# Order of the first loads, patch norms and splits in the prologue of a vision tower kernel

## The reference, cut to what matters

```python
pe = jax.lax.conv_general_dilated(pixel_values, conv_w, (PS, PS), 'VALID', ...)
red = grid.mean(axis=(3, 5)).reshape(b, C, hw).transpose(0, 2, 1)
win = grid.transpose(0, 2, 4, 3, 5, 1).reshape(b, hw, N, C)
q = _ln(red, la_ln_q_g, la_ln_q_b) @ la_wq
kv = _ln(win, la_ln_kv_g, la_ln_kv_b) @ la_wkv
...
local_out = red + agg @ la_proj_w + la_proj_b
```

## Time and profile before

| | us |
|---|---|
| median of 3 runs | 808.77 (808.05 to 809.29) |
| the profiled execution, its own time | 809.9 |
| its span in the profile | 807.9 |
| PE busy | 710.4 (88%) |
| DVE busy | 515.6 (64%) |
| POOL busy | 423.8 (52%) |
| ACT busy | 378.5 (47%) |

### The profile page before, as it was taken

The page is one execution under the profiler, slowest core; times in us unless marked ns, Lnnn a source line. Parts: engine busy times, 40 slices in busy tenths (PEclk is TensorE's granted clock), DMA queues, the critical chain, the costliest instruction groups (busy, mean ns, idle before and its releaser), DMA issues.

```text
span 807.9 us, 13117 instructions
## 1 busy us (share of the span) xinstructions
PE 710.4 (88%) x4247; PEld 608.9 (75%) x4247; DVE 515.6 (64%) x1230; ACT 378.5 (47%) x930; POOL 423.8 (52%) x360
## 2 busy tenths in 40 slices
PE   3669999999999999999847837999999999677797
PEld 3669998989889898655446736999999999444686
DVE  4567888778787787768988881223322233488957
ACT  3346666666576664643131332444444444156232
POOL 5555587676776853447949712343334432136640
PEclk9879999999999999999878967999999999689799
DMA  7943233323333202000011058898999992200001
GB/s 232 255 125 109 69 111 110 113 87 94 105 114 114 59 1 104 1 1 1 0 58 48 27 209 302 332 335 300 334 329 334 325 320 106 109 35 2 0 1 66
DMA packets 47064, 108.58 MB, mean 134 GB/s; under 512 B 5028, under 2 KB 24728, under 8 KB 39576
## 3 DMA queue, kind: packets, MB, share of 16 engines
q1 hardware_dynamic: 44408, 100.68, 37.3%
q0 software_dynamic: 2592, 7.10, 2.4%
HBM read 101.58 MB, written 6.17 MB: 133 GB/s over the span
## 4 chain that ended last, share of the span: by engine, by line
PE 74%; DVE 12%; SPq 3%; DMA 3%; POOL 3%; issue 2%; ACT 2%; DVEq 0%; ACTq 0%; POOLq 0%
PE banks L1703 12%; PE banks L1711 12%; PE banks L291 9%; PE banks L293 9%; PE banks L292 9%; PE banks L298 5%; PE banks L304 4%; PE banks L1311 3%; PE banks L1358 1%; DVE banks L1485 1%; PE banks L1285 1%; DVE a_o L1576 1%; DVE a_prod L1198 1%; PE banks L1341 1%; SPq L386 1%
## 5 line engine op out<-in xcount | busy, mean ns | idle before, releaser
L408 POOL TENSOR_TENSOR x_lo<-xraw,x_hi 128x512 fp32r<-128x512 f32 x81 | 105.6, 1304 | 99.7 <-ACT x_hi L402 99.6
L1794 ACT ACTIVATE hid<-banks,b 128x128 f32<-128x128 f32 x216 | 79.4, 368 | 110.4 <-PE banks L1703 110.4
L291 PE MATMUL banks<-wc_hi,x_hi 128*128 128x256 f32 x324 | 99.1, 306 | 19.4 <-POOL x_hi L411 13.3
L292 PE MATMUL banks<-wc_lo,x_hi 128*128 128x256 f32 x324 | 94.0, 290 | 0.0
L293 PE MATMUL banks<-wc_hi,x_lo 128*128 128x256 f32 x324 | 93.9, 290 | 0.0
L1959 DVE TENSOR_TENSOR res<-banks,xb 128x256 f32<-128x256 f32 x27 | 11.5, 425 | 127.3 <-PE banks L1711 127.3
L291 PEld LDWEIGHTS banks<-wc_hi,x_hi 128*128 128x128 f32 x324 | 64.3, 198 | 21.3 <-issue 13.5
L442 DVE BATCH_NORM_STATS2 stats<-banks 128x6 f32<-128x256 f32 x81 | 34.6, 428 | 69.4 <-ACT pe_sb L436 68.9
L291 PE MATMUL banks<-wkv_hi,xg_hi 128*128 128x512 f32 x162 | 70.9, 438 | 6.5 <-DVE xg_lo L503 6.3
L1832 POOL TENSOR_TENSOR y<-bve,mhalf 128x1 f32<-128x1 f32 x27 | 20.2, 747 | 105.7 <-DVE bve L1967 105.7
L402 ACT ACTIVATE x_hi<-xraw 128x768 fp32r<-128x768 f32 (+1 forms) x81 | 66.8, 830 | 12.1 <-DMA xraw<-in_x_rest 12.1
(11 more groups left out here) (331 smaller groups left out, 1828.1 us busy)
## 6 DMA issues: line engine op xcount, KB each, us to landing
w_raw<-in_w SPq DMA_DIRECT2D x28, 1024.0 KB, 6.6
xraw<-in_x_main SPq DMA_DIRECT2D x27, 768.0 KB
w1more<-in_w SPq DMA_DIRECT2D x13, 1024.0 KB, 6.0
w2more<-in_w SPq DMA_DIRECT2D x13, 1024.0 KB, 8.9
xraw<-in_x_rest SPq DMA_DIRECT2D x48, 96.0 KB
xraw<-in_x_rest SPq DMA_DIRECT2D x27, 114.0 KB
yl<-y_rows SPq DMA_DIRECT2D x2, 1028.0 KB, 6.9
a_w<-in_qkv_w SPq DMA_DIRECT2D x2, 768.0 KB, 5.4
```

What stands on the lines that cost most here:

```text
L291: pe.matmul(dst, a[0], b[0], start=start, stop=False)
L292: pe.matmul(dst, a[0], b[1], start=False, stop=False)
L408: pool.tensor_tensor(x_lo[:, i % RING_X, :], xraw[:, k, 0:KF].rearrange("p c b -> p (c b)"), x_hi[:, i % RING_X, 0:KF * P], ALU.subtract). ...
L1794: act.activation(hid[:, s % 2, fc, :], bank(fc % 2, 0, P), ACT.Gelu, bias=b1[:, bass.ds(e * FC + fc, 1)]).then_inc(sem("gelu_made"), 1)
```

## The change

It reorders instructions of all five engines in the prologue; none is added or left out.

- SP: the first group of window 1 (patches 9 to 11) is loaded ahead of the rows and the token weights, the other two behind them, unrolled; the loop starts at window 2.
- POOL: `early_std` stands behind the split of patch 8, `late_std` and the class row's power directly behind the split of patch 11 (before: behind those of 9 and 13).
- ACT: behind the rounding of patch 11 follow copies and norms in turn, the rounding of the first transpose and the norm of the sum; the roundings of patches 12 to 15 come behind all of that.
- PE: the rows product stands behind conv(10), not conv(9).
- DVE: the early shift stands behind `measure(5)`, not `measure(6)`; the first xg_lo stands ahead of the late shift; the rows sum and the class shift move into round 0, behind the second xg_lo.

```diff
@@ round_dve
                 if k == 0:
+                    if n == 0:
+                        dve.wait_ge(sem("kvb_done"), 3)
+                        dve.tensor_tensor(rows[:, 0:C], bank(7), rows[:, 0:C], ALU.add).then_inc(sem("kvb_made"), 1)
+                        dve.wait_ge(sem("kvb_made"), 2)
+                        shift_of(dve, CLASS_ROW, 0, 1, 1)
                     residual(dve, n)
@@ sync
+            load_x(sp, 1, 0)
             sp.dma_start(rows[:, :], d["rows"].broadcast_to([P, len(ROWS) * C])).then_inc(sem("tok_w_loaded"), 16)
...
-            with sp.Fori(1, NW) as n:
+            for g in range(1, NP // GRP):
+                load_x(sp, 1, g)
+            with sp.Fori(2, NW) as n:
@@ gpsimd
-                if i == 9:
+                if i == 8:
                     pool.wait_ge(sem("consts_made"), 1)
                     early_std(pool, 0)
-                if i == 13:
+                if i == LEAD:
                     late_std(pool, 0)
@@ tensor
-                if i == 9:
+                if i == LEAD - 1:
                     pe.wait_ge(sem("tok_w_loaded"), 128)
@@ scalar
-                if BEHIND <= i < LEAD - 1 + BEHIND:
+                if BEHIND <= i <= LEAD:
                     copy_pe(act, i - BEHIND)
@@
-                if i == 12:
+                if i == LEAD:
                     normalize_patch(act, 0)
+                    copy_pe(act, NP - 1)
                     normalize_patch(act, 1)
-                if i == 13:
                     split_xT_hi(act, 0)
-            normalize_red(act, 0)
+                    copy_pe(act, NP)
+                    normalize_red(act, 0)
@@ vector
-            for i in range(EARLY_KEYS, 7):
-                measure(dve, i)
+            measure(dve, EARLY_KEYS)
             shift_of(dve, 0, 0, EARLY_KEYS)
-            for i in range(7, NP):
+            for i in range(EARLY_KEYS + 1, NP):
                 measure(dve, i)
@@
+            split_xT_lo(dve, 0)
             shift_of(dve, 1, EARLY_KEYS, T)
-            shift_of(dve, CLASS_ROW, 0, 1, 1)
-            dve.wait_ge(sem("kvb_done"), 3)
-            dve.tensor_tensor(rows[:, 0:C], bank(7), rows[:, 0:C], ALU.add).then_inc(sem("kvb_made"), 1)
-            dve.wait_ge(sem("kvb_made"), 2)
-            split_xT_lo(dve, 0)
```

## The result

| | before | after |
|---|---|---|
| median of 5 runs each, same chip | 809.29 (808.05 to 810.55) | 801.70 (801.32 to 803.84) |
| the profiled execution, its own time | 809.9 | 801.3 |
| its span | 807.9 | 799.3 |

What follows compares the result with a forecast made beforehand. It took two TensorE stalls, 6.17 us (running sum) and 6.29 us (xg_lo), with slow clock behind, as the bound. 809.9 − 3.6 = 806.3, less 1.1, gave 805.2 us; range 798.5 to 808.2, the case's own 803 to 807.1.

Steps and rivals of the forecast that it cites:

- Step 1: Prologue loads: patches 9 to 11 issue from 16.5, land between 26 and 30.3; no ACT wait, patch 9 split at 28.0.
- Step 2: Before conv(7): second wkv_lo held by POOL's splits, conv(7) at 35.7 against 36.48, saving 0.8 us; idle stretch 5.4 us.
- The second is held through three splits: On DVE before conv(7): the second wkv_lo waits for three POOL splits, 1.64 us from one patch to the next, ending 34.9.
- short holds: Rival: DVE gets in after each single POOL instruction; conv(7) at 32.4, lead 9.6 us, time 799.2; chance 0.22.
- the sum: The forecast's added-up timeline: 3.6 us ahead at the third projection, PE's chain unchanged behind it, giving 805.2 us.
- Step 3: First projection: 11.1 us of PE work after conv(7), no wait for xg_lo(0); starts at 46.8, 7.1 us early.
- Step 4: project_q waits for redT behind ACT's four splits: starts 53.45 against 59.77, PE idle 3.4 us, slow clock charged 2.7.
- Step 5: DVE before the third projection: class shift held 3.9 us, xg_lo(2) at 59.2, PE there at 60.4, 3.6 us ahead.
- just covered: At the third projection: DVE's held work ends 59.2, before PE comes at 60.4; without slow clock it would bound by 1.5 us.
- Given back: Rival: the same stalls in new places, DVE held by patch 17 too; lead 0.8 to 1.6, time 807.2 to 808.0; chance 0.17.
- slower: Rival: POOL's splits run unbroken in round 0, class shift held 52.2 to 61.4; slower by 3.2 us, 812.0; chance 0.09.

Runs made afterwards that it cites:

- The change's second profile: The changed kernel itself, unaltered, measured again beside later kernels: 802.87 us, ratio 0.9926 to the kernel before.
- the kernel with the clock kept up: The changed kernel with 28 unread matmuls put on PE in its wait for redT ahead of the first project_q: 802.81 us, ratio 0.9921.
- the late roundings: The changed kernel with ACT's roundings of patches 14 to 16 moved behind the affine pair that makes redT: 804.05 us, ratio 0.9941.
- the order alone: The changed kernel with the old order on SyncE's load queue: 809.43 us, ratio 0.9997.
- load and order alone: Two runs: the kernel before with only SyncE's queue changed, 805.45 us; the changed kernel with SyncE's old queue, 809.43 us.
- the halved splits: The changed kernel with POOL's split of each patch cut into two instructions of 256 columns: 804.21 us, ratio 0.9939.

## Why the prediction was right, and where it was not

- **Step 1, loads: right.** No wait in front of patch 9's rounding at 27.26, and the early end of the range for the landing held: six issues took 3.2 us (16.43 to 19.64), and all had landed by 27.26. The weights held nobody up.
- **Step 2, conv 7: wrong.** "The second is held through three splits" is the step that failed. It was held through one: conv(7) at 31.44, not 35.7, and the idle stretch 1.73 us, not 5.4. That is 4.3 us of lead and the clock. The second wkv_lo lasted 1.77 us, so the prediction's own sign for short holds (0.7 to 2 us, and conv(7) before 33) is what came. The reason given for the long hold, that ACT has the next patches ready, was true (29.4 for patch 10) and did not decide it. Nor did the early shift meet an idle POOL: it was held 2.55 us, and conv(8) waited 1.17 us behind it, which the sum has at nothing. The Trainium skill (SBUF — State Buffer, Who interferes with whom), by which the loser waits for the whole instruction of the other, was nearer for wkv_lo; but the same profile has two shifts held through two splits, and the runs have holds of 4.31, 4.49 and 6.70 us. Neither rule is the whole of it.
- **Step 3, first projection: right in kind.** No idle in front. It stands 9.9 us behind conv(7), with 1.17 us of waiting in it; the 11.1 of the sum was taken from rows with some 6 us of slow clock (36 to 42 us in the kernel before, granted 0.50). The whole lead there is 12.6 us for 7.1.
- **Step 4, what is late next: the mechanism right, the size short.** redT behind the roundings, a PE pause of 4.56 us for the 3.4 forecast, the slow clock behind the pause. From the first projection to project_q it takes 8.13 us, not 6.65, and 1.64 of that is patch 15's load, a wait that the sum does not have: in the kernel before, ACT came to that patch at 46.8 and did not wait. Slow stretch: 49.43 to 56.03 is 6.60 for 4.27, so 2.33, charged at 2.7.
- **Step 5, DVE behind it: the mechanism right, the size over.** The class shift took 2.17 us, not 3.9, since POOL began its row at 42.8 for the 48.3 of the sum; it was held to the end of that row, as forecast. The last of DVE's work that the third projection needs (the product L530, ended 54.87) was 1.2 us ahead of it, and "just covered" stood on the same 1.2. The change's second profile, with a wait of 0.66 us there, and the kernel with the clock kept up show how thin that cover is.
- **The sum.** 8.0 us of lead for 3.6. Step 3's 5.5 us more, less 1.5 more for step 4, plus 0.4 for the clock give 4.4, which is the difference. Step 3's 5.5 are the 4.3 of step 2 and 1.2 that the faster clock gave, net of the wait of conv(8).
- **The rivals.** Short holds had conv(7) 32.4, first projection 40.8, project_q 47.45, lead 9.6, and is nearer in its steps; the measured time, 801.7, lies 3.5 under the forecast and 2.5 over this rival. What it had too small is the stretch from conv(7) to the first projection, 8.4 us for 9.86. Given back and slower did not come. Their mechanism did, in the late roundings, where the new hold ate a gain of 3.0 us.
- **What was luck.** That the time fell in the range is owed to the share of the range that was given to the short holds, and to two misses of opposite sign (4.3 us of lead too few in step 2, 1.5 us of cost too few in step 4). The gain was forecast at 3.6 us and measured at 7.6.

I had read the rule of holding from three rows of before and made it one of all or nothing. With a term that stands at two and three splits in such rows, and at one in others, both ends belong in the sum's middle value, not only in its range.

## What to carry to other kernels

Where each engine runs its list in order, a load is needed at the first instruction that waits for it, and everything behind that instruction needs it too: look at the queue behind the wait, and move load and list together, for either alone gave 3.4 us or nothing where both gave 7.6 (5.8 measured again). Between two engines that hold each other, work of the one that lies in a row costs more than the same work spread over the time: spreading GpSimd's splits, with the roundings of two patches moved into a wait of ScalarE, gave another 5.0 us. Moving the bias split of VectorE, which is held in either place, to where TensorE does not wait for it gave 1.5 us more by the profile (1.9 by the medians, whose intervals overlap). When a pause goes, ask who comes next: here ScalarE's string, then VectorE's row, then, up to 60 us, nobody.

## What the runs showed of the hardware that was not expected

- **Length of holds.** VectorE operations with all inputs and outputs in SBUF were held by GpSimd's splits (1.28 us each) for one (wkv_lo), two (2.55, 2.17), or three (4.31, 4.49); with splits of 0.73 us, for 6.70 us. The hold of wkv_lo (2.38) and that of the early shift (2.53 to 2.56) are the same, within 0.03 us, in the ten profiles that have both the changed load and the changed order there. Halving the splits made four holds shorter and two longer, so shorter instructions without a gap between them are no cure. Not every operation on SBUF was held: the mean and variance of a patch (L451, one input) took its 0.17 us at 31.31, in the middle of a split. In the second profile of the change the class shift took 1.44 us and the residual behind it 1.56, for 2.17 and 0.76 in the first. What decides how many splits pass is open. GpSimd's power on five columns (1.2 to 1.3 us) held nobody that the rows show: with the order alone the pair of wkv_lo ran beside it in its usual 1.29 us. Where VectorE got in, GpSimd's small L411 had grown from 0.46 to 0.64 to 1.2 us, a mark to look for.
- **The clock behind a short pause.** The same wait of 1.73 to 1.75 us in front of conv(7) stands in ten profiles (all but those of before, of load and order alone, and of the halved splits). In seven the granted clock stayed 1.00 behind it; in three it was at 0.50 to 0.65 for some 4 us. The change itself, in its first profile and in its second:

```profile
32.00:34.00 2.00, 1.49 (x13) 1.28 (x11) 2.00 (x2) 0.40 (x2) 2.00 (x4) 1.00 0.80 200
34.00:36.00 2.00, 1.34 (x11) 1.34 (x12) 1.43 (x6) 0.58 (x1) 0.34 (x1) 1.00 0.92 283
```

```profile
32.00:34.00 2.00, 1.57 (x8) 1.57 (x9) 2.00 (x4) 0.00 (x0) 2.00 (x4) 0.65 0.93 270
34.00:36.00 2.00, 2.00 (x10) 1.94 (x10) 1.68 (x4) 0.08 (x1) 1.33 (x2) 0.50 0.58 173
```

  It cost almost nothing: conv(7) to the first projection takes 9.86 us in the one and 10.01 in the other, since the slow convolution fills the 1.17 us that PE would have waited in front of conv(8). A slow clock costs only what no later wait would have taken.
